# Retimed step table, GpSimd last-layer normalisation, VectorE h3t copy and a new start-up order in a six-layer attention and FFN kernel on one Trainium2 core

## What is computed

```python
# D=6 layers, B=8 sequences, 512 tokens, 128 features, 16 heads of 8
def layer(h, p):
    q = (h @ wq.T + bq_).reshape(bh, sl, H, DH)
    k = (h @ wk.T + bk_).reshape(bh, sl, H, DH)
    scores = jnp.einsum('blhd,bmhd->bhlm', q, k) * inv_sqrt_d
    w_avg = jax.nn.softmax(scores, axis=-1).mean(axis=1)      # mean over the 16 heads
    new_w = jax.nn.softmax(CSCALE * w_avg + rel[None], axis=-1)
    sa = jnp.einsum('blm,bme->ble', new_w, h)
    h1 = _ln(h + sa, l1w, l1b)
    h2 = _ln(h1, l2w, l2b)
    ff = jax.nn.relu(h2 @ w1.T + b1_) @ w2.T + b2_
    return (_ln(h2 + ff, l3w, l3b), None)
x = x + attention_stack(layernorm(x))
x = x + ffn(layernorm(x))       # silu gate, two 512x512 gelu layers, back to 128
```

## Time and profile before

| | |
|---|---|
| median of 3 runs | 2819.93 us (2819.15 to 2830.39) |
| the profiled execution's own time | 2826.93 us |
| its span in the profile | 2824.8 us |
| start of the first exponential | 56.8 us |
| units 0 to 7 (layer 0) | about 53 us each |
| units 8 to 41 | mostly 50.2 us each |
| units 42 to 47 | about 54.3 us each |
| from the last exponential to the end | about 307 us |

### The profile page before, as it was taken

The page is one execution under the profiler, slowest core; times in us unless marked ns, Lnnn a source line. Parts: engine busy times, 40 slices in busy tenths (PEclk is TensorE's granted clock), DMA queues, the critical chain, the costliest instruction groups (busy, mean ns, idle before and its releaser), DMA issues.

```text
span 2824.8 us, 88963 instructions
## 1 busy us (share of the span) xinstructions
PE 2572.1 (91%) x35336; PEld 1241.6 (44%) x35336; DVE 2495.5 (88%) x5648; ACT 2465.0 (87%) x6785; POOL 1435.9 (51%) x1556
## 2 busy tenths in 40 slices
PE   3899999999999999999999999999999888978999
PEld 0344444444444444444444444443434434436776
DVE  5999999999999999999999999999999999984333
ACT  2999999999999999999999999999999989962222
POOL 3467765655556555565655655555555443444000
PEclk9999999999999999999999999999999999989999
DMA  5223434233242332424224242232332322210000
GB/s 116 50 54 72 76 76 72 47 59 50 53 63 63 60 49 53 63 47 76 48 53 63 42 80 49 55 61 39 65 65 51 54 47 35 36 43 27 15 19 19
DMA packets 98912, 152.87 MB, mean 54 GB/s; under 512 B 17856, under 2 KB 81088, under 8 KB 88896
## 3 DMA queue, kind: packets, MB, share of 16 engines
q1 hardware_dynamic: 98496, 147.18, 28.7%
HBM read 92.59 MB, written 41.94 MB: 48 GB/s over the span
## 4 chain that ended last, share of the span: by engine, by line
ACT 47%; PE 29%; DVE 14%; issue 8%; POOL 1%; DMA 1%; SPq 0%; DVEq 0%; ACTq 0%; POOLq 0%
ACT ex L792 39%; DVE negmax L639 9%; PE mean L935 7%; PE m L924 6%; PE sc L917 6%; PE sc L998 5%; ACT relu L837 3%; ACT ew L798 2%; DVE bn L603 1%; ACT h2t L801 1%; PE m L1007 1%; PE sc L985 1%; DVE mv L594 1%; ACT h3t L801 1%; ACT kf L778 1%
## 5 line engine op out<-in xcount | busy, mean ns | idle before, releaser
L792 ACT ACTIVATE ex<-sc,negmax 128x512 f32<-128x512 f32 x3072 | 2116.2, 770 | 87.9 <-DVE negmax L639 81.7
L639 DVE TENSOR_REDUCE negmax<-sc 128x1 f32<-128x512 f32 x3072 | 1946.0, 678 | 110.9 <-PE sc L917 106.5
L917 PE MATMUL sc<-kb,qb 96*32 96x512 bf16 x12288 | 1079.4, 386 | 160.0 <-ACT ex L792 117.2
L792 ACT ACTIVATION_READ_ACCUMULATOR ex<-sc,negmax 128x1 f32 x3072 | 886.6, 289 | 0.0
L935 PE MATMUL mean<-ex,rw 128*32 128x512 f32 x6144 | 819.9, 602 | 1.4 <-POOL rw L469 1.1
L917 PEld LDWEIGHTS sc<-kb,qb 96*32 96x32 bf16 x12288 | 344.5, 95 | 992.8 <-ACT ex L792 738.3
L469 POOL TENSOR_TENSOR rw<-sel_sb,zinv 128x256 f32<-128x256 f32 x384 | 236.7, 617 | 828.0 <-DVE zinv L645 828.0
L935 PEld LDWEIGHTS mean<-ex,rw 128*32 128x32 f32 x6144 | 209.1, 111 | 147.1 <-issue 57.6
L924 PE MATMUL m<-hc,pt 128*32 128x129 f32 x6144 | 208.5, 275 | 20.0 <-DVE pt L650 18.5
L924 PEld LDWEIGHTS m<-hc,pt 128*32 128x32 f32 x6144 | 173.1, 110 | 78.5 <-issue 33.8
L924 PE MATMUL m<-w_sb,relu 128*32 128x128 f32 x6144 | 203.4, 273 | 2.7 <-ACT relu L837 0.8
(11 more groups left out here) (94 smaller groups left out, 2485.3 us busy)
## 6 DMA issues: line engine op xcount, KB each, us to landing
kb<-qk_split SPq DMA_DIRECT2D x288, 128.0 KB
qb<-qk_split SPq DMA_DIRECT2D x576, 64.0 KB
qk_split<-qp SPq DMA_DIRECT2D x144, 128.0 KB, 1.8
qk_split<-kp SPq DMA_DIRECT2D x144, 128.0 KB, 1.8
hc<-hs SPq DMA_DIRECT2D x48, 256.0 KB, 6.6
xin<-x SPq DMA_DIRECT2D x16, 256.0 KB, 2.8
y_kept<-xin SPq DMA_DIRECT2D x8, 256.0 KB, 4.6
xin<-y_kept SPq DMA_DIRECT2D x8, 256.0 KB, 2.6
```

Of the source, the lines that this page charges most:

```text
L639: nc.vector.tensor_reduce(negmax[:, s % RT:s % RT + 1], sc[s % NS][:, :], AX, ALU.max, negate=True) \
L792: nc.scalar.activation(ex[:, s % ET, :], sc[s % NS][:, :], ACT.Exp, bias=negmax[:, c:c + 1], accum_out=zsum[:, c:c + 1]).then_inc(exp_read ...
L917: ins = nc.tensor.matmul(sc[s % NS][h * QS:h * QS + QS, :], qb[t % 2][:, h % 2, g, h // 2, r:r + QS], kb[t % 2][:, g, h // 2, :], start=Tr ...
```

## The change

1. The start: `qb` is filled before anything else on GpSimd, as f32 words; ScalarE runs one small exponential first (so the table load stands ahead of the first copy); the first sequence's `qp` stores and `qb` loads are issued from ScalarE's queue; GpSimd's second `power` and first `first_token` stand elsewhere.
2. The row order of `qb` and `kb` is new: term n's rows are every sixth partition and no longer a block of 16 (or 8).
3. `norm3_out` moves from ScalarE to VectorE, for the units of layers 0 to 4.
4. `last_apply` moves from VectorE (four instructions) to GpSimd (two); `net_first(0, 0)` now follows `last_spread`.
5. Nearly every number of `STEP` is moved by a few slots.

```diff
 STEP = {
-    "relative": (37, 51, 60, 78),
+    "relative": (39, 50, 61, 79),
-    "norm3_out": (142,),
+    "norm3_out": (143,),
-    "last_apply": (154,),
-    "last_turn": (159,),
+    "last_apply": (164,),
+    "last_turn": (165,),
...
+        def load_keys(queue, t):
+            for n, (_, ks) in enumerate(TERMS):
+                queue.dma_start(kb[t % 2][n:2 * ROWS:NTERM, :, :, :].rearrange("r g a s -> r (g a s)"),
+                                qk_dram[SEQ[t], 3 + ks, :, :].rearrange("(r g) s -> r (g s)", g=2 * NG)).then_inc(qk_loaded[t % 2], 16)
+
+        def load_queries(queue, t):
+            for n, (qs, _) in enumerate(TERMS):
+                for hh in range(2):
+                    queue.dma_start(qb[t % 2][ROWS * hh + n:ROWS * hh + ROWS:NTERM, hh, :, :, :].rearrange("r g a s -> r (g a s)"),
...
             def load_split(t):
-                for n, (qs, ks) in enumerate(TERMS):
-                    r = 2 * DH * n
-                    sp.dma_start(kb[par][r:r + 2 * DH, :, :, :].rearrange("r g a s -> r (g a s)"),
...
+                load_keys(sp, t)
+                if t > 0:
+                    load_queries(sp, t)
...
+            gp.memset(qb[0][:, :, :, :, :].rearrange("r h g a s -> r (h g a s)").bitcast(f32), 0.0).then_inc(filled, 1)
+            gp.memset(qb[1][:, :, :, :, :].rearrange("r h g a s -> r (h g a s)").bitcast(f32), 0.0).then_inc(filled, 1)
...
+                for t in due("last_apply", 0, g, j):
+                    y = OUTER[t]
+                    wait_later(gp, yt_ready, y)
+                    gp.wait_ge(veps_ready[3], B + y + 1)
+                    nc.gpsimd.tensor_tensor(xh3[:, :, :], xin[y % 2][:, :, :], mv[:, 3, :, 0:1].to_broadcast([P, NT, E]), ALU.subtract) \
+                        .then_inc(centered[3], 1)
+                    gp.wait_ge(centered[3], B - PRE + y + 1)
+                    gp.wait_ge(rstd_ready[3], B + y + 1)
+                    nc.gpsimd.tensor_tensor(xh3[:, :, :], xh3[:, :, :],
+                                            rstd[:, 3, :].rearrange("p (t a) -> p t a", a=1).to_broadcast([P, NT, E]),
+                                            ALU.mult).then_inc(xh_ready[3], 1)
...
+                for t in due("norm3_out", 0, g, j):
+                    dve.wait_ge(xh3t_ready, late_input(t) + 1)
+                    c = col[RUN[t] % 2]
+                    nc.vector.tensor_scalar(h3t[:, :], m1[:, :], c[:, C_W3:C_W3 + 1], c[:, C_BB3:C_BB3 + 1], ALU.mult, ALU.add) \
+                        .then_inc(ht_ready, 1)
...
-                for t in due("last_apply", 0, g, j):
-                    dve.wait_ge(rstd_ready[3], B + OUTER[t] + 1)
-                    for i in range(NT):
-                        apply(xh3, xin[OUTER[t] % 2][:, i, :], 3, i).then_inc(xh_ready[3], 1)
                     if t == U - 2:
                         net_first(0, 0)
...
+            act.wait_ge(filled, 1)
+            nc.scalar.activation(turn[:, :], one[:, :], ACT.Exp).then_inc(warmed, 1)
             act.wait_ge(qkw_loaded, 32)
             for b in range(PRE):
                 first_copy(b)
                 keys(b)
+                if b == 0:
+                    act.wait_ge(q_part, 4)
+                    for n in range(3):
+                        act.dma_start(qk_dram[0, n, :, :], qp[n][:, :]).then_inc(kept, 16)
+                    act.wait_ge(filled, 5)
+                    act.wait_ge(kept, KEPT)
+                    load_queries(act, 0)
...
-                for t in due("norm3_out", 0, g, j):
-                    act.wait_ge(xh3t_ready, late_input(t) + 1)
-                    affine(h3t, col[RUN[t] % 2], C_W3, ht_ready)
```

More of the change, by code:

```diff
@@ L23 @@
 TERMS = ((0, 0), (0, 1), (1, 0), (0, 2), (1, 1), (2, 0))
-ROWS = DH * len(TERMS)
+NTERM = len(TERMS)
+ROWS = DH * NTERM
 LOADS = 3 * len(TERMS)
@@ L76 @@
-    "queries": (155,),
+    "invert_sums": (11, 17, 27, 40, 42, 50, 61, 67),
+    "row_weights": (16, 17, 29, 48, 53, 61, 62, 68),
+    "sum_heads": (21, 23, 24, 27, 33, 38, 44, 44, 49, 52, 58, 59, 70, 71, 74, 76),
+    "exp_mean": (25, 44, 57, 73),
+    "transpose_mean": (30, 50, 61, 79),
+    "relative": (39, 50, 61, 79),
+    "attend": (42, 53, 77, 82),
+    "residual": (42, 56, 77, 81),
+    "stats0": (42, 62, 78, 82),
+    "spread": (82, 96, 135),
+    "power": (83, 101, 137),
+    "apply0": (83, 89),
@@ new lines @@
+    "norm1_weight": (89,),
+    "norm1_bias": (89,),
+    "stats1": (93, 93, 94, 95),
+    "apply1": (101, 105),
+    "norm2_turn": (105,),
+    "norm2_out": (102,),
+    "token_weight": (123,),
+    "token_bias": (128,),
+    "up": (106, 110, 120, 124),
+    "relu": (106, 108, 119, 122),
+    "down": (127, 129, 131, 133),
+    "add": (133,),
+    "stats2": (134, 134, 134, 134),
+    "apply2": (138, 138),
+    "norm3_turn": (143,),
+    "norm3_out": (143,),
+    "norm3_weight": (172,),
+    "norm3_bias": (185,),
@@ L77 @@
+    "project": (156, 158),
+    "queries": (156,),
     "keys": (157,),
[L78 to L81 removed]
+    "split_q": (175, 178, 181, 183),
+    "split_k": (174, 179, 181, 184),
+    "last_weight": (141,),
+    "last_bias": (142,),
     "last_add": (143,),
[L83 to L88 removed]
+    "last_stats": (148,),
@@ L89 @@
+    "last_spread": (155,),
+    "last_power": (155,),
+    "last_apply": (164,),
+    "last_turn": (165,),
+    "last_keep": (164,),
 }
@@ L452, in first_split @@
                 split_step(gp, nc.gpsimd, n, full, parts, part, first_input(b))
-            power(3, 1)
-            zero(0)
-            power(3, 2)
             for b in range(PRE):
-                first_token(b)
+                power(3, b + 1)
+                if b == 0:
+                    for i in range(2):
+                        ins = gp.memset(hc[i][:, :, E:E + 1], 1.0)
+                    ins.then_inc(filled, 1)
                 for n in range(4):
                     first_split(b, n, kf, kp, kf_ready, k_part)
-                if b == 0:
-                    zero(1)
+                first_token(b)
             gp.wait_ge(const_loaded, 32)
```

76 lines of the change are left out of this document (18 added, 58 removed).

## The result

The changed kernel takes 2792.03 us (median of 4 runs, 2790.66 to 2793.42); the kernel before, on the same chip, 2822.53 (2819.15 to 2830.39). The ratio is 0.9888, 95% interval 0.9865 to 0.9911. The profiled executions have spans of 2790.3 and 2824.8 us. Of all the runs in this document one stands apart as slow, the sixth of the kernel before with its key loads first (2978.10 us, at a mean granted clock of 0.846); no ratio uses it.

The account below looks back on a forecast made before the run. VectorE was taken to bound a unit's first half, ScalarE the second. Start -19.5, layer 0 +4, middle +12, last layer -16 and tail -5 sum to -24.5, from 2819.9 to 2795.4 us; likeliest case 2780 to 2808, wider range 2778 to 2818.

Parts of the forecast that it names:

- The two-bound unit: Middle unit of 50.17 us: VectorE bounds the first half, ScalarE the second; neither bounds the whole unit.
- The rival in which ScalarE's relief pays: Middle units: ScalarE, the busiest engine, is the bound, so -0.9 a unit; about 2755 us; chance 0.07.
- Middle units, +0.34 a unit: Units 8 to 41: `h3t` costs VectorE 0.66, new table shifts steps; 50.5 us a unit, +12 for 34 units.
- the hand-over: Middle unit: 0.95 us added to the largest sum of VectorE's and ScalarE's work, taken as the same after.
- the second rival: Loss in the middle eats the gain: `h3t` costs its full 0.66 in 40 units (+26); about 2817 us; chance 0.2.
- Layer 0, +0.6 a unit: Units 2 to 7, 53.02 us each: largest sum goes from 51.22 to 51.85, +4 in all.
- Last layer, -2.6 a unit: Units 42 to 47: VectorE loses four normalising instructions of 2.0 us, `zz` may shorten; -16, bounds -6 and -20.
- 0.65 that my sum leaves unexplained here: Last-layer unit: time beyond the largest sum and hand-over; if it went too, the gain would be -3.4 a unit.
- The start, -19.5: Start to first exponential: 56.78 us becomes 37.3, through earlier fill, table load, stores and loads; range -15 to -21.5.
- 12 at 0.33: Start: the longer of two load lists, twelve loads at 0.33 us each, done 4 us after 24.2, at 28.2.
- The tail, -5: After the last scores: `net_first` begins behind `last_spread`, up to 6 us earlier; -5, range 0 to -6.
- The irregular waits: Whole kernel: held to put the profiled execution 7 us above the runs' median, 2819.9; not attributed to the change.

Follow-up runs that it names:

- table-alone run: The kernel before with only the new numbers of STEP, `last_apply` still on VectorE at 158: 2827.17 us, ratio 1.0007.

## Why the prediction was right, and where it was not

The forecast, 2795.4, is 3.4 us over the measured 2792.0. From median to median the change is -30.5 us where I had -24.5, from span to span -34.5; the 2819.9 that I started from is 2.6 below the median of the later runs. So the sum is 6 to 10 us short, and part of its closeness is luck: in the middle a cost that was 7 us too small and a gain of 12.8 that I did not see cancel. The range "from start, tail and last layer at their ends" is not what its terms give either: all at their low ends come to about 2776, all at their high ends to about 2825, where I wrote 2780 to 2808.

- **The two-bound unit held.** VectorE bounds the first part, ScalarE the second; the windows cut at 16 us show it, and the two opposite moves of `h3t` confirm "worth nothing" on ScalarE and "it costs 0.66" on VectorE (0.63 to 0.66). The rival in which ScalarE's relief pays is excluded.
- **Middle units, +0.34 a unit: mis-sized.** Measured +0.57. `h3t` was right (0.63); "what the new table gives back" was 0.10, not 0.32. By the table-alone run my sum of 48.90 should have gone with 49.85; it was 50.07, so the hand-over grew from 0.95 to 1.17. I took it as constant. That was the second rival's argument, "differences of large sums", and it was right about this term.
- **Layer 0, +0.6 a unit: mis-sized.** Measured +0.15: `h3t` costs 0.66, but the table gives back 0.52 there; my sums gave it about none. And I took six units for units of 53.02 where the trace has four, 2 to 5; units 0 and 1, which I left out, became 2.1 us shorter together.
- **Last layer, -2.6 a unit: right** (-2.95), with `zz` at 0.34 as foreseen and GpSimd's instructions, 1.04 us each, in its free time. Of the normalisation's 2.0 us only 1.0 shows when it is moved alone, since under the new table it stands clear of GpSimd and takes 1.10. The blocking of up to 2.5 us by GpSimd that I priced did not eat the gain. The "0.65 that my sum leaves unexplained here" has a likely cause that I had before me: the 0.94 in the clock column of the earlier trace rows. It stood for 7 us at 0.51, and VectorE's wait of 0.99 came with it; no run separates the two.
- **The start, -19.5: mis-sized,** -15.7, inside its range. Every step came within 0.2 us up to GpSimd's split (16.66 for 16.5), the stores were issued by 23.4 for 22.8, and the loads began at 25.6 for 24.2. The step that failed is "12 at 0.33": with every sixth partition as destination a load takes 0.71 us to issue on ScalarE (8.49 for twelve) and 0.63 on SyncE. Adding that 4.5 (8.49 for 4.0) and the 1.4 us by which the first issue came later to the 34.6 that I had for the first maximum gives 40.5; measured 40.35. So the second sequence's chain did end last, as written.
- **The tail, -5: right** (-4.6 when the last unit's 3 are taken off 7.6), but loosely measured: from unit 47 to the end the kernel before and the four variants that leave its last steps alone took 357.7 to 365.7 us in their profiled executions. The reason may be incomplete: the clock differs there as well.
- **The irregular waits "that I do not attribute to the change": wrong.** They were 12.8 us of the middle and 2.4 more in unit 7 (53.19, now 50.74), the larger part of why units 0 to 7 came out 3.3 shorter instead of longer, and the change removed them. Both parts that remove them stood in the diff. I had seen the share of 1.04 at 116 GB/s in the earlier trace rows and used it for the start alone. This is the largest term that I missed. With the loads laid out and ordered as before, which brings these waits back, the ratio is 0.9991.

The Trainium skill (SBUF — State Buffer, "Door 1: The DMA port swizzle") says that a transfer's rate goes with how many of 16 ports its partitions reach. No run had shown it when I wrote; the share now agrees: rows spread over the partitions took 16.9% where blocks of 16 and 8 took 28.7%, for equal bytes. The Trainium skill (DMA: Bandwidth & Descriptors, "Issuing engines are not separate DMA queues") says that a second issuing engine saves issue time only. The runs agree: moving loads between ScalarE and SyncE changed the start by 0.8 and 2.1 us.

What stays open: why blocks and the alternation of key and query loads together make the packets of TensorE's instructions begin late. The late places recur: the waits end at 1083.67, 1754.93 and 2111.39 in the changed kernel with blocks and mixed issue, and at 1088.73, 1752.22 and 2106.03 in the table-only kernel. That fits packets that are due at fixed counts of instructions and meet the loads in some units only, but the trace does not name the DMA engine of a packet, and no run shows what it stands behind.

## What to carry to other kernels

When units of a periodic kernel differ, list their lengths first: nine long units among 34 told of a fault that no share of busy time shows, and its removal, with unit 7, was 15 of the 34.5 us of this change. When an engine stands without a semaphore to wait for, look at the packets of its instructions. Before moving a step to a "less busy" engine, cut the period into windows: the engine with nothing free in the window where the step stands pays in full, whatever its total. And test a change's parts alone: here a win of 1.1% held 29 us from the loads' layout and order, 13 from moving `last_apply`, and a loss of 25 from one moved instruction; with that one put back on its engine the win is 2%.

## What the runs showed of the hardware

- DMA issue time depends on the destination's rows: a key load between query loads takes SyncE 0.31 us into 16 neighbouring partitions and 0.51 into every sixth one; six in a row at the start 0.45 and 0.63 each; a query load on ScalarE 0.37 and 0.71.
- The same bytes kept the DMA engines busy for 28.7% in blocks and 16.9% spread. With blocks the first loads landed 13 us after the last issue, spread within 1.7 to 4.7.
- TensorE can stand 1 to 4 us in the middle of four equal matmuls with no semaphore to wait for, when a 16 KB packet of its instructions is late: 40 such waits in five kernels, all 193 to 195 records past a multiple of 256, each ending 1.4 to 2.2 us after a packet did.
- In each last-layer unit of the kernel before TensorE was granted 1.2 GHz for 3.4 or 6.8 us; in the unit shown it had been busy 2.43 of 4 and 4.79 of 6 us ahead of that, beside a full VectorE. In the changed kernel, busy 3.62 of 4 and 4.34 of 6 us at that place, it stayed at 2.4 GHz.
- The fill of 96x8192 bf16 took 6.92 us, the same bytes as 96x4096 f32 3.51: in these two fills GpSimd's time went with the elements, not the bytes. VectorE's four normalising instructions took 1.11 us with no fill beside them, 2.06 beside GpSimd's additions and 7.49 beside the fill.
